# Scaling the expert weights on GpSimd ahead of ScalarE's cast, in a two-layer gated cross-attention kernel

## What is computed

```python
x = x + tanh(g_xattn[0]) * L0_xattn(layernorm(x), ctx)     # cross attention, 32 keys
x = x + tanh(g_ffn[0])   * L0_ffn(layernorm(x))            # 8 experts take their top 64 tokens each
x = x + tanh(g_xattn[1]) * L1_xattn(layernorm(x), ctx)     # second cross attention, 16 heads
x = x + tanh(g_ffn[1])   * L1_ffn(layernorm(x))            # each token to 2 of 8 experts, SwiGLU, + shared expert
```

## Time and profile before

| | |
|---|---|
| median of 3 runs | 341.71 us (340.81 to 342.89) |
| the profiled execution | 344.11 us |
| its span, first to last instruction | 342.3 us |
| granted clock of PE, mean | 0.879 of full speed |
| busy: PE, DVE, ACT, POOL | 265.1, 223.1, 193.6, 160.8 us |

### The profile page before, as it was taken

How to read it: one execution, slowest core, us unless ns; L and a number is a source line. 1 busy time by engine, 2 the same in 40 slices (tenths; PEclk the granted TensorE clock), 3 DMA queues, 4 the chain that set the end, 5 groups by cost and what they waited for, 6 DMA issues and landing times.

```text
span 342.3 us, 7124 instructions
## 1 busy us (share of the span) xinstructions
PE 265.1 (77%) x2207; PEld 192.5 (56%) x2207; DVE 223.1 (65%) x687; ACT 193.6 (57%) x454; POOL 160.8 (47%) x208
## 2 busy tenths in 40 slices
PE   8797986998998969999886326038999999998620
PEld 4563442556775546868565212036988888887310
DVE  4377198976777557889996554251756556667366
ACT  3763899696776779768554241023744565565130
POOL 2414399902226275330157477700356566566612
PEclk9879999899999999999895556557999999999865
DMA  7880005599999930000011011121222113201083
GB/s 197 243 337 0 3 1 146 191 186 187 185 183 172 188 53 1 2 0 3 0 33 40 26 43 51 55 71 34 57 73 77 51 51 89 66 28 38 4 259 109
DMA packets 37795, 30.24 MB, mean 88 GB/s; under 512 B 3312, under 2 KB 35442, under 8 KB 37120
## 3 DMA queue, kind: packets, MB, share of 16 engines
q1 hardware_dynamic: 35120, 25.38, 34.3%
q0 software_dynamic: 2496, 4.26, 3.8%
q10 hardware_dynamic: 144, 0.15, 0.2%
HBM read 14.68 MB, written 16.00 MB: 90 GB/s over the span
## 4 chain that ended last, share of the span: by engine, by line
PE 44%; DVE 23%; issue 9%; ACT 8%; POOL 5%; another core or an unknown queue 4%; DMA 4%; SPq 1%; POOLq 0%; DVEq 0%; ACTq 0%
PE bank L1164 38%; POOL expert_rows L827 3%; DVE region_p L908 3%; DMA region_q<-expert_rows 2%; DVE region_k L894 2%; DMA wr<-in 2%; DVE region_x L1123 2%; DVE top L893 2%; PE bank L1387 1%; ACT region_k L702 1%; ACT x_hat L519 1%; DVE x L1149 1%; PE bank L1482 1%; PE bank L1374 1%
## 5 line engine op out<-in xcount | busy, mean ns | idle before, releaser
L1164 PE MATMUL bank<-w_high,region_k 128*128 (+1 forms) x308 | 35.5, 229 | 23.6 <-DVE region_k L1098 18.5
L1164 PE MATMUL bank<-w_scaled,w_high 128*128 128x256 f16 x276 | 48.4, 279 | 1.4 <-ACT w_scaled L697 1.0
L1164 PEld LDWEIGHTS bank<-w_high,region_k 128*128 128x128 f16 x308 | 27.1, 102 | 28.9 <-DVE region_k L1098 20.3
L827 POOL DMA_INDIRECT expert_rows<-region_k,slot_dest x24 | 25.9, 1078 | 36.4 <-DVE region_k L1131 27.8
L802 POOL DMA_INDIRECT dispatched_rows<-region_t,slot x32 | 31.6, 988 | 17.2 <-issue 9.2
L1134 DVE TENSOR_TENSOR region_k<-region_x,region_k 128x768 f16<-128x768 f32 x23 | 22.0, 958 | 25.3 <-ACT region_k L702 22.3
L1164 PE MATMUL bank<-w_scaled,w_low 128*128 128x256 f16 x138 | 38.5, 279 | 0.0
L697 ACT ACTIVATE w_scaled<-bank 128x512 f16<-128x512 f16 x23 | 13.7, 597 | 36.9 <-remote 23.2
L1164 PE MATMUL bank<-filler 128*128 128x512 f16 x94 | 28.7, 427 | 3.9 <-DVE region_k L894 2.4
L827 POOL DMA_INDIRECT expert_rows<-region_x,slot_dest x22 | 23.4, 1064 | 16.2 <-issue 11.4
L753 POOL TENSOR_TENSOR w_low<-w_scaled,w_high 128x512 f16<-128x512 f32 (+1 forms) x23 | 28.3, 1252 | 5.5 <-ACT w_high L531 5.3
(11 more groups left out here) (240 smaller groups left out, 719.9 us busy)
## 6 DMA issues: line engine op xcount, KB each, us to landing
dispatched_rows<-pad_rows SPq DMA_DIRECT2D x8, 1179.0 KB, 21.0
w_scaled<-in SPq DMA_DIRECT2D x5, 1024.0 KB, 8.1
w_scaled<-dispatched_rows SPq DMA_DIRECT2D x23, 131.0 KB
region_q<-expert_rows SPq DMA_DIRECT2D x3, 512.0 KB, 5.2
x<-in SPq DMA_DIRECT2D x4, 256.0 KB, 4.0
region_w<-in SPq DMA_DIRECT2D x2, 512.0 KB, 7.1
out<-x SPq DMA_DIRECT2D x3, 256.0 KB, 2.8
w_scaled<-in SPq DMA_DIRECT2D x1, 704.0 KB, 3.9
```

Of the source, the lines that this page charges most:

```text
L827: pool.indirect_dma_start(ytok, bass.IndirectOffsetOnAxis(dst[:, n, h:h + 1].bitcast(U32), 0), yv[n % 4][:, h * D:(h + 1) * D], None, boun ...
L1164: return pe.matmul(o, l, r, start=start, stop=stop)
```

## The change

Scaling by 256 goes from ACT to POOL. A new function `scale(i)` on POOL waits for the load (once for each four chunks), multiplies chunk i in place and counts up a new semaphore `w_scaled`. `split_high` on ACT now waits for that count and only casts. POOL's `scale` stands in two places of its queue: in the first stage two chunks behind each "rstd2" of batches 0 to 2 and chunks 6 to 11 behind that of batch 3; in the second cross attention at a new slot "scale" at t - 5.8, for chunks 12 to 22 (t = 0 to 10). ACT's tables and `split_low` are as before.

```diff
-C_POOL = {"rstd": -4.6, "early_low": -5.3, "low": -0.9, "rstd2": 6.5, "send": 12.5, "send2": 16.1}
+C_POOL = {"rstd": -4.6, "early_low": -5.3, "scale": -5.8, "low": -0.9, "rstd2": 6.5, "send": 12.5, "send2": 16.1}
...
-        a_link = sem("a_link")
+        w_scaled = sem("w_scaled")
...
             def split_high(i):
 
-                if i % WLOAD == 0:
-                    act.wait_ge(w_loaded[i // WLOAD], 16)
+                act.wait_ge(w_scaled, i + 1)
                 n = min(CH, W_END - i * CH)
                 r = slice(i % WRING * CH, i % WRING * CH + n)
-                act.activation(wf[:, r], wf[:, r], ACT.Copy, scale=WS).then_inc(a_link, 1)
-                act.wait_ge(a_link, i + 1)
                 act.activation(wh[:, i * CH:i * CH + n], wf[:, r], ACT.Copy).then_inc(w_high_done, 1)
...
+            def scale(i):
+
+                if i % WLOAD == 0:
+                    pool.wait_ge(w_loaded[i // WLOAD], 16)
+                n = min(CH, W_END - i * CH)
+                r = slice(i % WRING * CH, i % WRING * CH + n)
+                pool.tensor_scalar(wf[:, r], wf[:, r], WS, 0.0, ALU.mult, ALU.add).then_inc(w_scaled, 1)
+
...
                 elif stage == "rstd2":
                     rstd_of(b, sel_stats, sel_rstd)
+                    for i in range(2 * b, 2 * b + 2 if b < B - 1 else EARLY):
+                        scale(i)
...
                 elif stage == ("early_low" if t < C_FIRST else "low") and EARLY + t < CHUNKS:
                     split_low(EARLY + t)
+                elif stage == "scale" and EARLY <= EARLY + t < CHUNKS:
+                    scale(EARLY + t)
```

## The result

The changed kernel takes **347.65 us** (median of 4 runs, 344.77 to 348.73) against 341.58 us for the kernel before (median of 4, 340.81 to 342.89). The ratio is 1.0158, with a 95% interval of 1.0109 to 1.0207: slower by 5.4 us. 345.9 was forecast, in a range of 343.3 to 348.2. The profiled execution took 348.38 us, its span 346.6 us (before: 344.11 and 342.3). Some executions of any of these kernels are slower at a lower granted clock; the medians in this document are of all executions, the ratios leave those out.

A forecast was written before the change was run, and what follows sets the result against it. No single engine bound the kernel; the tiles ran in a loop of PE's scores and DVE's shift. 3.2 + 0.2 + 0.3 + 1.0 - 0.5 = +4.2 us on 341.71 gave 345.9 us, range 343.3 to 348.2.

The forecast's parts named there:

- The wait: Start of second cross attention: cast 14 waits for POOL's scale 14, delaying the keys and first normalisation; 3.2 us.
- The price of a scale: One POOL scaling of 512 columns, extrapolated from rows of 128 and 4 columns: 0.64 us, range 0.30 to 1.16.
- the rival of the slow price: POOL scaling takes 1.16 us, with longer stands of DVE at the port lock: 347.2 to 348.2 us; chance 0.13.
- The stand at L951: Before the second cross attention's tiles: scale 12 on POOL stands in front of DVE's L951; 0.2 us (0 to 0.7).
- At L880: First stage: DVE's L880 stands beside POOL's scales 0 and 1, through the shared port lock; 0.3 us (0 to 0.6).
- The clock: First tiles of second cross attention: PE idles, probably falls to half clock and slows score matmuls; 1.0 us, bounds 0 and 2.0.
- The relief in the tiles: Second cross attention's tiles: ACT loses eight scalings between tiles, giving back 0.5 us; bounds 0 and 5.0.
- The rival in which ACT bounds the tiles: Second cross attention: eight chunks' relief counts in full, 5.0 us instead of 0.5, giving 341.4 us; chance 0.06.
- The top-token search: ACT loses 12 scalings, 7.4 us, but POOL's low halves and DVE's compares do not move; gain counted as 0.
- The rival of shifted stalls: End of the second cross attention: unattributed gaps fall elsewhere, 2 to 4 us either way around 345.9; chance 0.10.

The follow-up runs named there:

- experiment 1: Changed kernel with scale 14 moved ahead of the rstd of batch 0 in POOL's queue; 342.39 us, ratio 1.0015 to the kernel before.
- experiment 3: Only the second half of the change: against the kernel before, POOL scales chunks 12 to 22, ACT still 0 to 11; 348.83 us, ratio 1.0270.
- experiment 8: Changed kernel with one more POOL instruction, a scaling of 1024 spare columns, right ahead of scale 14; 350.75 us, ratio 1.0182 to the kernel before.
- experiment 2: Only the first half of the change: against the kernel before, POOL scales chunks 0 to 11, ACT still 12 to 22; 341.91 us, ratio 1.0045.
- experiment 11: The changed kernel, unaltered, profiled and timed once more; 346.10 us beside 340.05 for the kernel before, ratio 1.0203.
- experiment 4: Changed kernel with 15 filler matmuls on PE ahead of its wait for the first normalised tile; 344.27 us, ratio 1.0112 to the kernel before.

## Why the prediction was right, step by step

- **The wait** (3.2 forecast): 3.3 in both profiles of the changed kernel. Each link has the length it was given: low 13 1.15 us, scale 14 0.62, cast 14 0.63, the keys 1.06. Experiments 1, 3 and 8 show it as the cause.
- **The price of a scale** (0.64, from two shorter rows of the same kind): 0.62. The upper bound, taken from the two-input instruction, was far off, and the rival of the slow price falls.
- **The stand at L951** (0.2): L960 took 0.41 us beside scale 12 in place of 0.29; from the slots to the rstd it is 0.1 us. **At L880** (0.3): 0.49 in place of 0.23 in the changed kernel, but 0.23 and 0.24 in experiments 2 and 1. The forecast put it on the boundary of two scales. In the trace it began 0.15 us into scale 0 (24.19 us, POOL) and ended with it; in experiment 1 it started ahead of the scales, in experiment 2 less than 0.2 us before scale 0 ended, and both took the usual time. How long it stands thus depends on when the batch arrives. Both rows, L889 and L960, are of the changed kernel:

```profile
24.34 0.49 DVE L889 TENSOR_SCALAR r_z<-r_z,tanh_gates 128x4 f32<-128x4 f32 x1
...
112.51 0.41 DVE L960 TENSOR_SCALAR region_k<-region_k,slot_rz 128x128 f32<-128x128 f32 x1
```

- **The clock** (1.0, bounds 0 and 2.0): the mechanism was right, the size not. It measured 2.5 and 1.2 us. The term charged 0.9 us for one tile; in the first profile two tiles' scores ran at 1.92 us, and a scatter beside them (2.39 us at 133.12, where 1.95 is usual) came on top. The upper bound of 2.0 was too low by 0.5, and by more for experiment 8. What failed is the length given to the slow stretch.
- **The relief in the tiles** (0.5, bounds 0 and 5.0): 0.2 in both profiles of the changed kernel, and 0.2 with the scaling gone from all engines. The chain's single piece of 0.52 us was not gained in full; that the loop of PE and DVE stood behind ACT fits the waits of the earlier trace rows, but was not tested by itself. The rival in which ACT bounds the tiles falls.
- **The top-token search** (0): confirmed, by 6.77 us of idle time on ACT and the same 14.2 us on DVE ahead of the compares.
- **The rival of shifted stalls** (0.10, either way): it did happen, as -2.6 us in the tail of the profiles, beside the forecast and not in place of it. The forecast had left it out of its sum.

The sum of the first profile's steps is 3.3 + 2.5 + 0.1 + 0.3 - 0.2 - 2.6 = 3.4 us. With the 0.9 us of the loads' variation it is 4.3, just what the two spans differ by (346.6 and 342.3). That this is near the 4.2 of the forecast is luck: the clock cost 1.5 us more than forecast, and the tail gave back 2.6 us that were in no term. The timed medians differ by 6.1 us, and the ratio makes 5.4 us. Without the tail's gain the steps sum to 6.0. **What stays open** is this tail: two programs with the same work behind the last tile differ by 2.6 us there, repeatably in the profiles (38.98, 39.16 and 39.07 for three that leave POOL as before and ACT's early scaling too; 36.40, 36.13, 36.40, 36.86, 36.45 for five with POOL scales, in the order changed kernel, experiments 11, 2, 3 and 4; 37.85 for experiment 1; 41.94 for experiment 8, whose POOL queue has one instruction more ahead of scale 14). About 1.3 us of it have arisen at the addition 13 us behind the last maximum, the rest at the slot numbers of the last batch. At both DVE waits longer in the kernel before, for something that the profile doesn't name ("remote"): total us, times, longest, first before, then changed.

```profile
DVE z_inv L990 <- remote: 2.2, 1, 2.2
DVE rank_row L1048 <- remote: 3.4, 1, 3.4
```

```profile
DVE z_inv L999 <- PE bank L1173: 0.8, 1, 0.8
DVE rank_row L1057 <- remote: 2.6, 1, 2.6
```

Small changes ahead of it on POOL or on ACT shift it. What it waits for was not found, nor whether the timed executions have the gain at all.

No version beat both kernels. Experiment 1 has the time of the kernel before, to within 0.7%.

## What to carry to other kernels

When work moves to another engine, write out both queues around it and look at what the new waiting instruction stands in front of. Here 0.6 us of work cost 5 us because it stood behind POOL's rstd and a low half, and in front of its user's successors, which needed that rstd; two places earlier in POOL's queue it cost nothing that the times show. Add PE's clock to the price of a new idle stretch like this one of 3.5 us, and count relief on an engine only where the chain has no other loop beside it.

## What the runs showed of the hardware

- Behind the stretch of 3.5 us with PE all but idle ahead of the first tile (4.5 us in experiment 8) the granted clock fell to 0.50 in all four profiles without fillers there (the changed kernel twice, experiments 3 and 8). Half clock then lasted some 3.4 us in one, 7 in two and 10 in experiment 8. 15 filler matmuls (3.40 us busy) in the stretch kept it at 1.00.
- POOL scales 512 columns of float32 in 0.62 us and 1024 in 1.04 us: 0.82 ns for each further column. The subtraction with two inputs takes 1.15 us for 512 columns, almost twice as long as the scaling.
- A short DVE instruction that began inside a POOL scaling and stood, ended with it: 0.49 us instead of 0.23 at 24.34, 0.41 instead of 0.29 at 112.51.
- Behind the last tiles, while POOL issued indirect stores, ACT stood for 4.1 us and DVE for 3.7 in the kernel before, 3.9 and 3.6 in the changed one; PE, DVE and ACT stood all at once for 2.2 and 2.0 us of that. The whole stretch took 36.1 to 39.2 us with the same work in it, and moved with instructions added or removed over 100 us earlier.
